# GpSimd's order of scatters and gathers in the expert loop: first half's scatter, both gathers, second half's scatter

## The reference

```python
x = x + attn(layernorm(x), delta, alpha, beta, gamma, omega)   # a long convolution per channel, as a recurrence
x = x + ffn(layernorm(x), expert_weights, expert_indices, w1_A, w1_B, w2_A, w2_B)
# ffn: each expert index in a row of expert_indices (TOPK = 2, E = 8) sends the token's row through
h = gelu(xr @ w1A[e].T @ w1B[e]);  ye = h @ w2A[e].T @ w2B[e]  # RANK = 64, FF = 2048
y = zeros((T, hs)).at[tok].add(flat_w[order][:, None] * out)   # T = 4096 tokens, each written by its experts
```

## Time and profile before

| | |
|---|---|
| median of 3 runs | 1104.19 us (1102.78 to 1105.65) |
| the profiled execution | 1103.91 us, its span 1101.7 us |
| PE clock granted, mean | 0.94 |
| first gather of the expert stage | 386.2 us from the span's start |
| the 24 tiles of the hardware loop | 463.04 to 734.18 us, 271.14 us |

### The profile page before, as it was taken

How to read it: one execution, slowest core, us unless ns; L and a number is a source line. 1 busy time by engine, 2 the same in 40 slices (tenths; PEclk the granted TensorE clock), 3 DMA queues, 4 the chain that set the end, 5 groups by cost and what they waited for, 6 DMA issues and landing times. The chain is left out here.

```text
span 1101.7 us, 31975 instructions
## 1 busy us (share of the span) xinstructions
PE 889.2 (81%) x11186; PEld 732.8 (67%) x11186; DVE 809.6 (73%) x1350; ACT 764.0 (69%) x1124; POOL 577.0 (52%) x641
## 2 busy tenths in 40 slices
PE   2770588879868878999999999999779888886981
PEld 1540576767757757777777777778657777775771
DVE  7978897988969534567665666766668889796891
ACT  3872698989969744656565565656359989896990
POOL 5445886878855143556566565655554333232330
PEclk9995799999989989999999999999889999899996
DMA  8999999999999989999999888899949999999976
GB/s 301 344 400 364 228 255 223 260 250 287 315 280 307 277 194 281 235 282 283 258 293 221 251 211 240 213 238 241 235 106 277 244 245 264 253 315 296 305 169 153
DMA packets 390535, 286.21 MB, mean 260 GB/s; under 512 B 124784, under 2 KB 338434, under 8 KB 389948
## 3 DMA queue, kind: packets, MB, share of 16 engines
q1 hardware_dynamic: 345980, 211.67, 70.9%
q0 software_dynamic: 17952, 34.42, 15.3%
q10 hardware_dynamic: 26528, 39.14, 10.0%
HBM read 195.57 MB, written 98.77 MB: 267 GB/s over the span
## 5 line engine op out<-in xcount | busy, mean ns | idle before, releaser
L1565 PE MATMUL ps<-xn,wb 128*128 128x128 f32 x2048 | 275.4, 290 | 0.0
L1565 PEld LDWEIGHTS ps<-xn,wb 128*128 128x128 f32 x2048 | 250.3, 200 | 17.3 <-issue 2.8
L622 POOL TENSOR_TENSOR cen<-xb,mean 128x512 f32<-128x512 f32 x128 | 142.3, 1113 | 221.9 <-DVE state L1371 151.0
L1344 DVE TENSOR_TENSOR xn<-cen,rstd 128x1024 f32<-128x1024 f32 x128 | 176.0, 1375 | 43.9 <-POOL cen L622 33.9
L1552 PE MATMUL ps<-xn,near 128*32 128x128 f32 x2048 | 86.5, 288 | 116.5 <-DVE xn L1344 71.9
L1355 DVE TENSOR_TENSOR xb<-xb,ps 128x1024 f32 (+1 forms) x128 | 152.8, 1194 | 9.4 <-PE ps L1577 9.4
L1027 ACT ACTIVATE wb<-wide 32x1024 f32<-32x1024 f32 x126 | 144.5, 1147 | 15.5 <-DMA wide<-taps_d 12.9
L1129 ACT ACTIVATE cen<-ps 128x1024 f32<-128x1024 f32 x110 | 109.5, 1024 | 64.2 <-PE ps L1675 42.0
L1552 PEld LDWEIGHTS ps<-xn,near 128*32 128x32 f32 x2048 | 52.0, 112 | 140.4 <-issue 72.2
L1675 PE MATMUL ps<-carry,wb 64*128 64x256 f32 x1024 | 127.9, 390 | 6.7 <-issue 4.1
L1675 PEld LDWEIGHTS ps<-carry,wb 64*128 64x128 f32 x1024 | 99.8, 191 | 37.2 <-issue 24.4
(11 more groups left out here) (211 smaller groups left out, 1454.1 us busy)
## 6 DMA issues: line engine op xcount, KB each, us to landing
xb<-L_attn_x SPq DMA_DIRECT2D x160, 512.0 KB, 9.2
out<-xb SPq DMA_DIRECT2D x72, 512.0 KB, 6.5
xb<-L_attn_x ACTq DMA_DIRECT2D x128, 256.0 KB
out<-xb SPq DMA_DIRECT2D x88, 256.0 KB, 4.5
wb<-L_ffn_w_B SPq DMA_DIRECT2D x78, 256.0 KB
wide<-taps_d SPq DMA_DIRECT2D x63, 256.0 KB
dk<-decay_d SPq DMA_DIRECT2D x63, 128.0 KB
out<-y_d SPq DMA_DIRECT2D x4, 1536.0 KB
```

Source lines behind the costliest of these rows:

```text
L622: pool.tensor_tensor(cen[:, k, 0:QB // 2].rearrange("p b r d -> p r b d"), unit_view(pool, g, i, k)[:, :, 0:UC // 2] .rearrange("p r (b d) ...
L1344: dve.tensor_tensor(xn[:, k].rearrange("p (b d) r -> p b d r", d=2), cen[:, k].rearrange("p b r d -> p b d r"), rstd[:, g * P:(g + 1) * P] ...
L1565: ins = pe.matmul(ps[:, QB * k + b, d * P:(d + 1) * P], wb[:, h, k * QB + b, d, :], xn[:, k, 2 * b + d, :], start=(b > 0 and d == 0), stop ...
```

## The change

In the hardware loop alone (tiles 5 to 28, where `q` is not a Python integer), GpSimd's order within a tile becomes: deviation, the wait for the landed scatters, the first half's scatter, both gathers, the second half's scatter, the copies of columns. Before, both halves were scattered ahead of the gathers. Tiles 0 to 4 and 29 to 38 keep the order they had. Waits and buffers are the same.

```diff
-            def scatter(q, m, j=None):
+            def scatter(q, m, j=None, parts=None):
 
                 before = 16 * ((q + 1) // 2)
                 now(pool, before, tok(q) + 1, tok(q) + 2)
                 pool.wait_ge(s_const, 1)
                 for h in range(halves(q - 1)):
                     wait(pool, s_s[2 * (1 - m % 2) + h], before)
-                for h in range(halves(q)):
+                for h in range(halves(q) if parts is None else parts):
                     scatter_half(q, m, h, j)
...
                 if not isinstance(q, int):
-                    scatter(q - 3, (m + 1) % 4, (m + 3) % 4)
+                    scatter(q - 3, (m + 1) % 4, (m + 3) % 4, 1)
...
                 if is_in(q, NQ - 3):
                     gather(q + 3, 1 - k, None if isinstance(q, int) else (m + 3) % 4)
+                if not isinstance(q, int):
+                    scatter_half(q - 3, (m + 1) % 4, 1, (m + 3) % 4)
                 if isinstance(q, int) and q == ROW0:
                     picked(0, 0)
```

## The result

| | before | after |
|---|---|---|
| median, runs on the same chip | 1103.49 us (1102.03 to 1105.65, 4 runs) | 1126.88 us (1122.22 to 1130.57, 4 runs) |
| ratio | | 1.0208 (1.0165 to 1.0251) |
| the profiled execution, its span | 1103.91, 1101.7 us | 1125.81, 1123.6 us |
| 24 loop tiles | 271.14 us, 11.30 each | 295.34 us, 12.31 each |

The changed kernel is 2.1% slower. The forecast was 1117 us, with 1103 to 1140 around it.

What follows compares the result with a forecast made beforehand. PE was taken to pace the loop at 11.30 us a tile. 24 rings of 12.0 us lose 24 x 0.70 = 16.8 us, less 3.8 swallowed leaves 13, on 1104.2: 1117 us, range 1103 to 1140.

Steps and rivals of the forecast that it cites:

- The bound of the kernel before: Expert loop: PE sets the 11.30 us tile; the first half's wait for the previous tile's landings has 1.0 us to spare.
- The gathers, worth 0: Loop gathers moved ahead of one scatter: PE's transposes already hold them and nobody needs them earlier, so 0 gain.
- rival 4: Loop: earlier gathers, once GpSimd is late, give PE back 5 us; 1099 us, chance 0.04.
- The ring: GpSimd and its queue: next first half waits for this tile's second-half landing, closing a loop of 5.8 us plus issue-to-landing time.
- the wake: GpSimd in the loop: 0.84 us from a landing to the start of the first half waiting for it.
- ring 12.0: Each of 24 loop tiles takes 12.0 us against 11.30, so GpSimd falls 16.8 us behind.
- Early 12.4, late 11.7: Ring nearer 12.4 us in the loop's first ten tiles, where DMA engines lack spare time, and nearer 11.7 later.
- 3.8 us swallowed: GpSimd's lateness before PE suffers: 2.7 us free before the deviation is wanted, 1.1 more before PE's transposes.
- 1 and 2: Loop landing waits: ring stays under the tile (0.17), or landings are much quicker in an unobstructed queue (0.06); both 1104 us.
- S: Second half's time from issue to landing in the loop, behind two gathers: 5.9 to 6.3 us, bounded by 5.1 and 7.4.
- The quick release of the earlier trace: Tail scatter issued at 804.55 released the next at 808.34; taken as support for an 8.8 us ring, chance 0.06.
- The long ring: Loop: second half still takes 7.4 us to land, ring 13.2, costing 42 us; 1148 us, chance 0.15.

Runs made afterwards that it cites:

- e2: Kernel before, old order, odd tiles scattering into a scratch array so a first half waits for the tile two before: 1106.54 us, ratio 0.9981.
- e5: Kernel before, with both loop gathers also waiting until DVE has begun its first copy of the next rank result: 1102.01 us, ratio 0.9976.
- e10: Kernel before, with both loop gathers waiting for all three of DVE's copies of the rank result: 1106.64 us, ratio 1.0011.
- e6: e1 with the second half's scatter also held until DVE's copy of the rank result: 1107.61 us, ratio 1.0016 to before.
- e8: Changed kernel with the second half's scatter between the two gathers, so one gather ahead of it and one behind: 1112.42 us, ratio 1.006 to before.
- e1: Changed kernel, odd tiles scattering into a scratch array so a first half waits for the tile two before: 1135.81 us, ratio 1.0249 to before.
- e7: e5 with three small GpSimd compute operations filling the place the gathers left: 1100.3 us, ratio 0.9934 to before.
- e3: Changed kernel with one small GpSimd operation added ahead of the second half's scatter in the loop: 1125.88 us, ratio 1.0169 to before.
- e9: Changed kernel with the new order in only every second loop tile, the old order in the others: 1118.89 us, ratio 1.0144 to before.
- e4: Changed kernel with one small GpSimd operation added behind the second half's scatter in the loop: 1130.25 us, ratio 1.0196 to before.

## Why the prediction came out as it did

*The bound of the kernel before* was right in what it watched: the wait for the landing had 1.0 us to spare by the sum (0.95 by the records), and e2 shows that taking it away changes nothing. It was incomplete. PE's 11.3 us held a gather's hold-up already (lag 1.43), which none of the views I had read names; whether it costs anything there is not shown, since e5 and e10 have no such lag and no gain.

*The gathers, worth 0.* Right. The first gather starts 0.30 us after h0's end (564.78 less 564.48) instead of the 0.6 forecast, since GpSimd is late by then and PE's transposes are over, and no one gained by it: rival 4 (1099 us) did not come.

*The ring.* Its mechanism was right and binds in all 24 tiles; removing it and the hold-up (e6) gives the time back. Its parts, beside what they measured:
- h1 goes out at X + 4.7 by the median (forecast 5.0), and the wake is 0.95 (forecast 0.84, from a wait for PE).
- The queue serves in order, as forecast: landings in order of issue at 6.9, 8.8, 10.2 and 11.4. But the steps failed in size and cancelled each other. The first half was to be done at X + 4.8 and took 6.9, though alone in the queue until X + 2.0; the two gathers took 3.3 (forecast 3.5), and the second half 1.2 more where 2.55 to 3.0 were forecast. The end, 11.4, is near the upper end of the forecast's 10.9 to 11.3, so that it fits is luck in part. The transfers of one tile seem to overlap and share the time; they don't add up like issues on an engine. e8 shows the same: one transfer less ahead of h1 brings its landing forward by 0.4, not by 1.75.
- So the term "ring 12.0" measured 12.3 (12.31 by the mean): 24 x 0.31 is 7.4 us more than the sum had. The 17 tiles without a large lag took 11.9, near the forecast's value; the seven others, 13.4, brought the mean to 12.3.
- *Early 12.4, late 11.7* did not come: the third to the tenth tile took 11.9 by the mean, the last 14 took 12.1. Where the share of the DMA engines is lowest (0.73, 730.99 to 744.64) the ring is among the longest. The first two tiles took 16.0 and 13.8, 5.9 us above two rings of 12.0; I had allowed under 1 us for the start. In the first of them h1 goes out at X + 7.15, since the first gather, at X + 4.45, is held back by PE's transposes.

*3.8 us swallowed* held inside the loop and failed behind it. The sum was 24 x 0.70 = 16.8 less 3.8. Measured, GpSimd's loop grew by 24.2 and the span by 21.9, and 1.4 of the difference lies ahead of the loop, where the two kernels are the same: 0.9 at most was swallowed in the end. At the loop's end, against the kernel before, GpSimd's first half is 22.8 us late and PE's transposes 19.8, so 3.0 us were swallowed by then. PE's rank multiplications stay 19.8 late up to those at 767.5 in the kernel before, and from the next ones (774.0) on they are 21.2 to 22.3 late. The tail, where GpSimd was to catch up in waits of 2.9 to 4.7 us and to cost PE 1 us at most, gave 2 us of the 3 back. The last two of those three waits are rings too. In the tail of the changed kernel,

```profile
756.99 1.68 POOL L586 DMA_INDIRECT out<-lag,slot_s  x1 [2.64 <-issue]
...
767.27 1.65 POOL L586 DMA_INDIRECT out<-carry,slot_s  x1 [3.12 <-issue]
...
777.45 1.65 POOL L586 DMA_INDIRECT out<-carry,slot_s  x1 [3.67 <-issue]
```

each first half comes 0.92 to 0.95 us after the landing that it waits for (the one after these 1.27). In the kernel before the same holds for the first halves at 754.62, 776.55 and 785.56 (0.92 to 0.93), while the one at 765.63, for which the view names ACT, comes 1.27 after it. For the two in the earlier trace rows the view says "issue". An engine that waits for a landing can't catch up; I had read a wait as slack without asking what released it. Together the ring term (7.4 us) and the swallowed part (2.9) make up the 10 us between the sum and the measured time, and 5.9 of the 7.4 are in the first two tiles.

*The hold-up* was in no part of the prediction. The measured time lies in the forecast's range all the same, and that is luck in part: in the changed kernel every first half waits for the landing, but the seven tiles in which an issue also holds the rank copy up are 1.6 us longer than the rest, and no run parts the two there. Without the ring the loop is 33 us longer than before (e1), so the loss was coming by one way or the other.

*The rivals.* 1 and 2 asked for rings under 11.3; three single ones were (10.54, 10.78 and 10.84, with S of 4.8 to 5.2), and 21 were not. The quick release of the earlier trace rows had no like in the loop: the queue's packets between 804.5 and 808 hold 0.00 MB, so that scatter wrote nothing. The long ring (13.2; its own sum, 1104.2 + 42, gives 1146 us and not 1148) was met by three tiles from 13.5 to 13.8, beside the first, and not by the mean. The Trainium skill's page "DMA: Bandwidth & Descriptors", section "Anatomy of one DMA — SWDGE (gpsimd) path" (2.0 us plus bytes at 436 GB/s, an estimate of 2.6 us for a half), is far from the landings of the loop: 4.8 us is the lowest median of a scatter in any run, 4.1 its shortest single one, and the line's scatters took 5.1 to 8.0. Near it come only the scatters at the tail's end that write nothing, 2.8 to 3.0 us. The same page of the Trainium skill says in "Queues, rings and completion order", there of DMAs that SP and ACT issue, that a completion's increment lands only after every earlier write of that DMA engine, across its queues. If that holds for GpSimd's too, a first half's landing would move with other traffic, as it does between 4.8 and 6.9, but no run here takes the other traffic away.

## What to carry to other kernels

Before moving an asynchronous transfer on an in-order engine, close every ring it stands in: who waits for its landing, and when will the landing be if the queue first works off what is now ahead of it; then compare with the stage's own pace, and give the loop no slack back that is itself a wait for a landing. Take such landings from the semaphore's records, since the view may put the wait down to another engine or to "issue". And when removing a wait moves an issue, look at what PE does during that issue, and tile by tile, since a median hides it: e1 had no ring and was the slowest kernel of all.

## What the runs showed of the hardware

- The issue of an indirect DMA by GpSimd (1.0 to 1.1 us for a gather, 1.6 for a scatter) can hold up PE, and DVE and ACT after it, where it falls on the short multiplications before a hand-over: in the changed kernel 5 matmuls start in a second half's issue of 1.63 us against 27 in a first half's of 1.67 (means of 24), and the copy that waits starts as the issue ends. Three ordinary operations of 2.6 us in all, in the same place, do nothing of the kind (e7). What is shared was not found.
- From its issue a first half lands after 4.8 to 4.9 us (before, e1, e2), 5.8 (e6), 6.0 to 6.2 (e3, e5, e7, e9, e10), 6.4 to 6.5 (e8, e4) or 6.9 (after; all medians). That goes neither with what is issued behind it nor with the order as such; where the tile's other traffic stands at that moment may be it, which no run tells apart.
- After a landing GpSimd needs 0.92 to 1.05 us until the first half that waits for it starts, and 0.8 at the tail's end, where it waits for one scatter in place of two.
